# ScalarE instead of VectorE normalises the rows of x in a fused cross-attention and feed-forward kernel

## The reference, cut to what matters

```python
# x: (4, 512, 512) f32; ctx: (4, 512, 256); the two weights of the FFN: (2048, 512) and (512, 2048)
def xattn(teacher_logits, teacher_features, Wq, bq, Wk, bk):
    query = einsum('bnc,dc->bnd', teacher_features, Wq) + bq
    key   = einsum('bnc,dc->bnd', teacher_features, Wk) + bk
    attention = softmax(einsum('bnd,bmd->bnm', query, key), axis=-1)
    return einsum('bln,bmn->blm', teacher_logits, attention)

x = x + xattn(layernorm(x), ctx, Wq, bq, Wk, bk)     # layernorm: (x - mean) / sqrt(var + 1e-5), by row
x = x + ffn(layernorm(x), ln_w, ln_b, W1, b1, W2, b2)
# ffn: LayerNorm, linear 512->2048, GELU, linear 2048->512, residual. Both linears quantise their two
# operands to int8 with one power-of-two scale per block of 32 (MXINT8); results rounded to bf16.
```

## Time and profile before

| | |
|---|---|
| median of three runs | 303.73 us (303.25 to 304.36) |
| the profiled execution, its own time | 303.7 us |
| its span, first to last instruction | 301.5 us (2.2 us lie around it) |
| mean granted TensorE clock | 0.928 of full speed |
| busy: TensorE / VectorE / ScalarE / GpSimd | 234.2 / 261.8 / 182.9 / 61.6 us |
| instructions: VectorE / ScalarE / GpSimd | 393 / 295 / 67 |
| chain that ended last | VectorE 41%, TensorE 25%, ScalarE 15%, issue 8%, DMA 7%, GpSimd 3% |

### The profile page before, as it was taken

One profiled execution on the slowest core, in us unless ns is written; L12 is line 12 of the kernel. 1 busy time (PEld: TensorE's weight loads), 2 busy tenths in 40 slices (PEclk: granted clock), 3 DMA queues, 4 the chain that ended last, 5 costly groups with the idle time before them and its releaser, 6 DMA issues.

```text
span 301.5 us, 3213 instructions
## 1 busy us (share of the span) xinstructions
PE 234.2 (78%) x916; PEld 102.1 (34%) x916; DVE 261.8 (87%) x393; ACT 182.9 (61%) x295; POOL 61.6 (20%) x67
## 2 busy tenths in 40 slices
PE   1575519985987069708399979999999989999974
PEld 0323204441432023203144434444444434444431
DVE  4379999999977999979978959599999999998942
ACT  2129517876999069967666499966556554555401
POOL 4240244027305813057310120300000000000000
PEclk9999969999899759975689999999999999999978
DMA  6997993989837936293540314655353555564961
GB/s 182 386 383 236 221 207 77 248 212 218 213 70 177 205 73 194 51 176 67 107 89 17 58 28 87 125 122 115 62 110 80 122 122 122 128 131 94 154 156 70
DMA packets 102765, 42.92 MB, mean 142 GB/s; under 512 B 93532, under 2 KB 95840, under 8 KB 102240
## 3 DMA queue, kind: packets, MB, share of 16 engines
q1 hardware_dynamic: 99024, 32.78, 52.0%
q10 hardware_dynamic: 3728, 9.99, 10.2%
HBM read 15.48 MB, written 4.19 MB: 65 GB/s over the span
## 4 chain that ended last, share of the span: by engine, by line
DVE 41%; PE 25%; ACT 15%; issue 8%; DMA 7%; POOL 3%; SPq 0%; ACTq 0%; DVEq 0%; POOLq 0%
DVE amax L753 10%; PE ps L713 9%; PE ps L701 7%; DVE xn L930 5%; DMA xhl<-pf 3%; DVE hq L947 3%; DVE vw L942 3%; DMA cx<-in_ctx 3%; PE ps L658 3%; DVE pf L854 2%; DVE nmax L909 2%; DVE wquant L800 2%; DVE phl L923 2%; PE ps L698 2%; DVE stats L899 2%
## 5 line engine op out<-in xcount | busy, mean ns | idle before, releaser
L701 PE MATMUL ps<-w1T,cxT 128*128 128x512 bf16 x256 | 67.5, 387 | 0.0
L658 PE MATMUL ps<-pT,xT 128*128 128x512 f16 x192 | 49.4, 412 | 14.7 <-DMA pT<-phl 12.1
L713 PE MATMUL ps<-w2T,xhl 128*128 128x512 bf16 x256 | 59.6, 387 | 0.0
L564 ACT ACTIVATE wst<-ps 128x1024 bf16<-128x1024 f32 x32 | 32.3, 1019 | 34.6 <-PE ps L701 34.6
L753 DVE TENSOR_REDUCE amax<-phl 128x64 f32<-128x2048 bf16 x16 | 36.5, 2282 | 9.0 <-ACT phl L568 9.0
L646 PE MATMUL ps<-qkT 128*128 128x512 f32 x32 | 18.5, 683 | 25.2 <-ACT pf L445 18.9
L701 PEld LDWEIGHTS ps<-w1T,cxT 128*128 128x128 bf16 x256 | 25.4, 99 | 31.7 <-issue 3.1
L713 PEld LDWEIGHTS ps<-w2T,xhl 128*128 128x128 bf16 x256 | 25.5, 100 | 31.0 <-issue 2.2
L658 PEld LDWEIGHTS ps<-pT,xT 128*128 128x128 f16 x192 | 19.7, 104 | 47.8 <-issue 30.9
L389 POOL TENSOR_TENSOR wst<-wst,mxi 128x2048 f32<-128x2048 f32 x8 | 30.4, 3796 | 20.0 <-DVE mxi L772 20.0
L568 ACT ACTIVATE phl<-wst 128x2048 bf16<-128x2048 bf16 x16 | 30.6, 1910 | 1.3
(11 more groups left out here) (76 smaller groups left out, 340.7 us busy)
## 6 DMA issues: line engine op xcount, KB each, us to landing
wst<-in_L_ffn_W ACTq DMA_DIRECT2D x8, 1024.0 KB, 6.2
out_x<-wst SPq DMA_DIRECT2D x16, 256.0 KB, 2.7
xs<-in_x SPq DMA_DIRECT2D x3, 1024.0 KB, 13.9
cx<-in_ctx SPq DMA_DIRECT2D x4, 512.0 KB, 7.5
xs<-in_x ACTq DMA_DIRECT2D x1, 1024.0 KB, 8.6
xhl<-pf SPq DMA_TRANSPOSE x17, 4.3
lnw<-in_L_ffn_ln_w ACTq DMA_DIRECT2D x1, 256.0 KB, 15.8
lnb<-in_L_ffn_ln_b ACTq DMA_DIRECT2D x1, 256.0 KB, 16.8
```

The source lines that it names most:

```text
L564: act.activation(ys[:, k, 1024 * g:1024 * g + 1024], ps_y[:, 2 * g:2 * g + 2, :], ACT.Copy)\
L658: pe.matmul(ps_pv[:, t % 2, :], xT[:, t, NT * a + n, :], pT[:, :, NT * c + n, :], start=(s == 0), stop=False)
L701: last = pe.matmul(ps_y[:, c, :], h1T[:, k, t, :], w1T[:, 4 * c:4 * c + 4, t, :], start=False, stop=(t == KT - 1))
L713: last = pe.matmul(ps_z[:, k, :], h2T[:, k, t, :], w2T[:, t, :], start=False, stop=(t == FT - 1))
```

## The change

`normalise` moves from VectorE to ScalarE, where it stands behind `x_high` of its tile, and `x_high` no longer rounds `xn`: it computes the normalised value itself, from `xs`, with the same scale and offset, and writes it in f16. ScalarE's form is scale * x + offset, so GpSimd gets two small operations more per batch, in `factors_x`: mx = -mean, and offx = mx * rx. `x_low` still subtracts the two, and now waits for `normalise` on ScalarE as well. `x_high` waits for the offset once per front instead of for each `xn`. VectorE loses 16 instructions, ScalarE gains 16, and the 16 of `x_high` get two operands more.

```diff
--- before.py
+++ after.py
@@ -95,6 +95,8 @@
         ms = sb("ms", [P, LT], F32)
         rs = sb("rs", [P, 3, LT, 2], F32)
         rx = sb("rx", [P, LT], F32)
+        mx = sb("mx", [P, LT], F32)
+        offx = sb("offx", [P, LT], F32)
         off = sb("off", [P, LT], F32)
         squares = sb("squares", [P, 2, H], BF16)
         half = sb("half", [P, LT], F32)
@@ -167,7 +169,7 @@
         rsr = [sem(f"rsr{n}") for n in range(3)]
         nm, off_rdy = sem("nm"), sem("off_rdy")
         v_mean, v_mean2, v_ms = sem("v_mean"), sem("v_mean2"), sem("v_ms")
-        rx_rdy = sem("rx_rdy")
+        rx_rdy, mx_rdy, offx_rdy = sem("rx_rdy"), sem("mx_rdy"), sem("offx_rdy")
         w_u = [sem("w1_u"), sem("w2_u")]
 
         xT_rdy = [sem(f"xT_rdy{t}") for t in range(LT)]
@@ -350,9 +352,13 @@
                 wait_alone(pool, mvr, LT * (b + 1), pool_gate)
                 wait_alone(pool, xn_rdy, LT * b, pool_gate)
                 pool.tensor_scalar(rs[:, 0, :, 0], mv[:, :, 1], EPS, None, ALU.add).then_inc(ve[0], 1)
+                pool.tensor_scalar(mx[:, :], mv[:, :, 0], -1.0, None, ALU.mult).then_inc(mx_rdy, 1)
                 rsqrt(0, b)
                 wait_alone(pool, rsr[0], b + 1, pool_gate)
                 pool.tensor_scalar(rx[:, :], rs[:, 0, :, 1], XSCALE, None, ALU.mult).then_inc(rx_rdy, 1)
+                wait_alone(pool, mx_rdy, b + 1, pool_gate)
+                wait_alone(pool, rx_rdy, b + 1, pool_gate)
+                pool.tensor_tensor(offx[:, :], mx[:, :], rx[:, :], ALU.mult).then_inc(offx_rdy, 1)
 
             def mean_x1(b):
                 wait_alone(pool, x1_rdy, LT * (b + 1), pool_gate)
@@ -452,9 +458,16 @@
                    .then_inc(p_hi, 1)
 
             def x_high(b, t):
-                act.wait_ge(xn_rdy, b * LT + (t + 1))
+                if t == 0:
+                    act.wait_ge(offx_rdy, b + 1)
                 wait(act, xT_rdy[t], 16 * b)
-                act.activation(xhl[:, t, 0, :], xn[:, t % 2, :], ACT.Copy).then_inc(x_hi, 1)
+                act.activation(xhl[:, t, 0, :], xs[:, LT * b + t, :], ACT.Identity, scale=rx[:, t:t + 1],
+                               bias=offx[:, t:t + 1]).then_inc(x_hi, 1)
+
+            def normalise(b, t):
+                wait(act, x_lo, b * LT + (t - 1))
+                act.activation(xn[:, t % 2, :], xs[:, LT * b + t, :], ACT.Identity, scale=rx[:, t:t + 1],
+                               bias=offx[:, t:t + 1]).then_inc(xn_rdy, 1)
 
             def order_w(a, u):
 
@@ -513,6 +526,7 @@
                     if t < NT:
                         exp(front, t)
                         x_high(front, t)
+                        normalise(front, t)
                     if t > 0:
                         p_high(front, t - 1)
                     if b is not None and t > 1:
@@ -923,15 +937,9 @@
                 dve.scalar_tensor_tensor(phl[:, t, 1, :], pf[:, t, :], rinv[:, t, 1:2], phl[:, t, 0, :],
                                          ALU.mult, ALU.subtract).then_inc(p_lo, 1)
 
-            def normalise(b, t):
-                if t == 0:
-                    dve.wait_ge(rx_rdy, b + 1)
-                wait_alone(dve, x_lo, b * LT + (t - 1), dve_gate)
-                dve.tensor_scalar(xn[:, t % 2, :], xs[:, LT * b + t, :], mv[:, t, 0:1], rx[:, t:t + 1],
-                                  ALU.subtract, ALU.mult).then_inc(xn_rdy, 1)
-
             def x_low(b, t):
                 dve.wait_ge(x_hi, b * LT + (t + 1))
+                dve.wait_ge(xn_rdy, b * LT + (t + 1))
                 dve.tensor_tensor(xhl[:, t, 1, :], xn[:, t % 2, :], xhl[:, t, 0, :], ALU.subtract)\
                    .then_inc(x_lo, 1)
 
@@ -953,12 +961,10 @@
 
 
                 negmax(b, 0)
-                normalise(b, 0)
                 if w1 is not None:
                     w_amax(W1, w1)
 
                 negmax(b, 1)
-                normalise(b, 1)
                 recip(b, 0)
                 if w1 is not None:
                     w_power(W1, w1)
@@ -972,7 +978,6 @@
                     h1_amax(h1)
 
                 negmax(b, 2)
-                normalise(b, 2)
                 recip(b, 1)
                 if h1 is not None:
                     h1_power(h1)
@@ -987,7 +992,6 @@
                     w_clip(W2, w2)
 
                 negmax(b, 3)
-                normalise(b, 3)
                 recip(b, 2)
                 if h1 is not None:
                     h1_over(h1)
```

## The result

The changed kernel takes **311.59 us** (median of four runs, 311.33 to 311.88), the one before 303.49 beside it: a ratio of 1.0273, 95% interval 1.0229 to 1.0316. Run again beside the experiments it took 309.82 us, 1.0229 (1.0175 to 1.0283). The prediction had 311.0 us and a range of 307.5 to 314.0.

A forecast was written before the change was run, and what follows sets the result against it. The prediction took ScalarE to bound the fronts' ends: 2.3 + (2.3 to 3.2) + 2.25 = 6.85 to 7.75 us, taken as 7.3 on 303.7, gave 311.0 us. The range was 307.5 to 314.0.

The forecast's parts named there:

- The sign and the size: Whole kernel: slower, with chance 0.87, by 7.3 us, to 311.0 us.
- ScalarE, 0.90 us a tile: ScalarE in the fronts: x_high and normalise at 0.71 us each cost 0.90 us more a tile, 14.4 for the kernel.
- Front 0, +2.3: Front 0: ScalarE's 3.6 us more, less 1.3 of waits, make p_high(2) and the statistics 2.3 us later.
- Front 3, +2.25: Front 3: ScalarE's last sums, and times_w behind them, come 2.25 us later, from +0.45 and +1.8.
- Fronts 1 and 2, +2.3 to +3.2 together: Fronts 1 and 2: p_high(2) of front 2 1.7 to 2.6 us late, plus 0.6 for GpSimd, delaying front 3.
- The open choice in front 2: Front 2: whether w_power waits for GpSimd's multiplication, putting p_high(0) at 74.9 instead of 74.0; the middle was taken.
- GpSimd, +0.6 behind front 2: Behind front 2: mx and offx stand on the path ahead of x1_square and cost 0.6 us; elsewhere nothing.
- VectorE's relief is worth nothing: Fronts: VectorE losing 16 x 0.54 us and the stalls gains nothing where the fronts end on ScalarE.
- VectorE is the bound: Rival, chance 0.08: fronts end on VectorE's own work, so 8.6 to 18.7 us go, giving 295.1 to 285.0 us.
- Everything is paid: Rival, 0.05 for nearly this: no idle time covers ScalarE's 14.4 us or GpSimd's 4 x 0.6, giving 320.5 us.

The follow-up runs named there:

- Only where it pays: Kernel before, but in front 3 alone ScalarE does x_high and normalise from xs, ahead of the first exp; mx, offx for batch 3 alone: 301.35 us, 0.9954.
- ScalarE relieved: Changed kernel with ScalarE's x_high and normalise cut to 32 of 512 columns, and x_low subtracting from xs: 300.76 us, 0.9932 of the kernel before.
- GpSimd alone: Kernel before with only GpSimd's mx and offx added, read by nobody: 304.30 us, 1.0036.
- high part alone: Kernel before with x_high computed from xs and GpSimd's mx and offx added, normalise staying on VectorE: 304.76 us against 303.14, 1.0044.
- VectorE's order: "Only where it pays" with, in VectorE's front 2, normalise(1) right behind normalise(0) and recip_scaled(0) ahead of w_power: 299.72 us against 303.40, 0.9894.
- The same, with fronts 0 and 2 as before: Kernel before, but in fronts 1 and 3 ScalarE does normalise and x_high from xs, all ahead of the first exp: 302.49 us against 303.27, 0.9965.

## Why the prediction was right, by its steps

**The sign and the size** were right: +7.3 us forecast, +7.26 measured in the fronts, 311.0 against 311.59. The agreement to 0.04 us is luck: the medians differ by 8.1 us in the first measurement and 6.4 in the second, and the forecast was worked out from the very profile that the fronts are compared with. The other runs bear the reason out: ScalarE's work taken away (-0.6 instead of +7.3), moved to idle time (front 3 from +1.9 to -1.8), and split into halves (7.4 of it with `normalise`).

**ScalarE, 0.90 us a tile:** right; 0.70 and 0.71 us per activation.

**Front 0, +2.3:** measured +2.27, and dependent on that profile. The wait of 0.99 us for `xn` that I counted as cover was there because GpSimd's multiplication had caught the first `normalise`. With that out of the way front 0 of before took 20.97 us, and the change's 24.52, the same in three other profiles of it to 0.01, is 3.55 longer: nearly all of the 3.6 that I had before taking off the waits. **Front 3, +2.25:** ScalarE's last sums came 2.2 us later in the front. `times_w` moved by 1.93 only, since the first of `factors_v` ran into a `p_low` of VectorE before and took 0.87 us, and now it starts half a microsecond after the sums and takes 0.23 (at 136.81).

**Fronts 1 and 2, +2.3 to +3.2 together:** measured 3.06 against the one profile of before, and 1.8 against fronts 1 and 2 of "Only where it pays"; the split is as uncertain. I had 0.45 for front 1; it is 0.95. The statistics came 0.62 later, and then `negmax` waited 0.24 us for TensorE, whose fourth `values` had waited 0.56 us for `x_plus`(1) (at 61.89, the row above). I had seen that this moves, and had carried it on ScalarE alone, not to the next `negmax`. But front 1 of before is 24.66 to 25.28 us long in profiles of unaltered orders, so half a microsecond here can be scatter.

**The open choice in front 2** fell on the upper side: `w_power` came after the start of the multiplication (74.34 against 74.11) and was held for 3.46 us. `p_high`(0) waited 0.56 for it, and 0.67 us came back with the order changed. `p_high`(2) is 2.6 us late against the start of front 1, the upper end of 1.7 to 2.6. The Trainium skill (SBUF — State Buffer, "SBUF: two separate sides") had this right: the rows of before showed only `w_mult` and `normalise` under the multiplication, these also show `w_power`, and `p_low` with its two SBUF inputs, both held until the end. The middle that I took was half a microsecond too low there.

**GpSimd, +0.6 behind front 2:** +0.50 alone. In the change it was 0.46: `offx` took 0.89 us (98.16) where 0.2 is usual, in the place of a later operation that had met VectorE's `p_low` before.

**VectorE's relief is worth nothing:** right for the change, in all four fronts, though for two reasons. In fronts 0, 2 and 3 ScalarE bounds them. In front 1 TensorE stands behind ScalarE, which I did not name: 2.57 us of wait in the run with ScalarE relieved. Where ScalarE's work is out of the way too, the relief is worth something: front 3 was 0.8 us shorter with it cut down, and 1.8 to 2.2 with it moved ahead. VectorE's busy time fell by 7.6 us, not by 9 to 15, as nearly all of the stall time moved.

**The rivals.** "VectorE is the bound" had VectorE's share of 87% behind it, and it would have been 8.6 to 18.7 us faster. The most that was found by taking ScalarE's load away is 0.6 us in the fronts. "Everything is paid" fell too: 14.4 us of ScalarE, and half of it met idle time.

## What to carry to other kernels

Before work is moved off the busiest engine, look at which instruction ends each stage and count what the receiving engine has to do in front of it; a share of the span says nothing about that, and free time of the receiver counts only if it lies ahead of that instruction. Here 16 activations cost 7.3 us in the middle of the fronts, and four of them with their `x_high`, put into ScalarE's 8 us of idle time ahead of the last front, gained 2.2. In front 1 the same gained 0.2 at most, as TensorE held the next front up. Where an engine is held by another, moving the victim away hands the stall to the next instruction; it goes only if something that nobody waits for stands there.

## What the runs showed of the hardware that was not expected

- Operations of one element per partition were not held by GpSimd's multiplication: `recip_scaled` took 0.15 us at 50.57, inside the one from 49.95 to 53.59, while `w_power` with 64 elements was held for 3.46 us.
- TensorE's clock in front 1 moves fronts 1 and 2 from profile to profile. It was idle for 4.5 to 6.1 us before its first matmul inside the front, and in the first 3 us of the front the granted clock was 0.50 of 2.4 GHz, which is 1.2 GHz, in the five profiles that have the order of before in front 1. From there on it rose earlier or later: in the next 5 us it was 0.86 on average in the kernel before and 0.62 in the one with front 3 alone. The front's first 12 matmuls of `values` took from 3.26 to 4.43 us. Kernel before, and front 3 alone:

```profile
45.70 3.26 PE L658 MATMUL ps<-pT,xT 128*128 128x512 f16 x12
```

```profile
46.16 4.43 PE L710 MATMUL ps<-pT,xT 128*128 128x512 f16 x12
```

In these five profiles (`values` at 3.26, 3.26, 3.87, 4.43 and 4.09 us, in the order before, GpSimd alone, high part alone, front 3 alone, and VectorE's order) ScalarE's first `exp` of front 2 starts 22.34 or 22.35 us plus that time after the start of front 1. So TensorE, through the queries and keys of the next batch and `x1_square` behind them, sets when ScalarE begins front 2 in these kernels. In the change it does not: with 4.00 and 4.26 us, `exp` starts after 27.11 both times.
- The last 20 us differ by 1.7 us between executions of kernels that are alike there. TensorE waits about 2 us for a transpose, and then its 16 matmuls take 5.30 or 3.62 us. TensorE, timeline, kernel before and the run with front 3 alone:

```profile
288.01 0.39 PE L709 MATMUL ps<-wqk,ones 128*128 128x512 bf16 x1 [1.96 <-DMA xhl<-pf]
...
288.24 5.30 PE L713 MATMUL ps<-w2T,xhl 128*128 128x512 bf16 x16
```

```profile
287.59 0.39 PE L761 MATMUL ps<-wqk,ones 128*128 128x512 bf16 x1 [1.93 <-DMA xhl<-pf]
...
287.81 3.62 PE L765 MATMUL ps<-w2T,xhl 128*128 128x512 bf16 x16
```

The granted clock of the last 20 us was 0.86 of 2.4 GHz in the first, a mean in which a part stood at 1.2 GHz (0.50 from 290.0 to 291.5), and 0.98 in the second, after idle times of 1.96 and 1.93 us. In "The same, with fronts 0 and 2 as before" it did not fall after 2.01 us, so the profiles in which it fell and those in which it didn't can't be told apart by this idle time. With ScalarE relieved the wait was 1.16 us, and the clock stayed at 0.99. A difference of half a per cent between two executions can be this alone. The fronts' lengths leave it out; they repeat to 0.01 us in the two profiles of the change, but only to about 0.6 us, and 1.9 in front 0, in kernels with the orders of before.
